# A decoder layer's attended values divided through row-step DMAs instead of PE transposes, with every engine's order rewritten

## What is computed

```python
attn = jax.nn.softmax(scores, axis=-1)                       # self: 112 keys, cross: 375 keys
out = jnp.einsum('bhqk,bkhd->bqhd', attn, V).reshape(b, s, H * hd)
x1 = _layernorm(x + out @ Wo.T + bo)                         # after the self attention
...
xq = fp4_quant_dequant(x2); wq = fp4_quant_dequant(w)        # blocks of 16, scale = max|x| / 6
```

## Time and profile before

| what | value |
|---|---|
| median of 3 runs | 660.07 us (658.95 to 660.67) |
| the profiled execution | 659.02 us |
| its span | 657.2 us |
| granted PE clock, mean | 0.97 of full speed |
| busy: PE, DVE, ACT, POOL | 583.8, 494.2, 292.3, 222.1 us |
| DMA moved | 69.61 MB, mean 106 GB/s |
| packets | 65568 |

### The profile page before, as it was taken

One profiled execution on the slowest core, in us unless ns is written; L12 is line 12 of the kernel. 1 busy time (PEld: TensorE's weight loads), 2 busy tenths in 40 slices (PEclk: granted clock), 3 DMA queues, 4 the chain that ended last, 5 costly groups with the idle time before them and its releaser, 6 DMA issues.

```text
span 657.2 us, 16127 instructions
## 1 busy us (share of the span) xinstructions
PE 583.8 (89%) x5602; PEld 372.0 (57%) x5602; DVE 494.2 (75%) x1475; ACT 292.3 (44%) x703; POOL 222.1 (34%) x280
## 2 busy tenths in 40 slices
PE   3677898898999999999999999989999999887874
PEld 3444566465566666666665656565666655554542
DVE  3598889876969687786969685668788696968662
ACT  1333365554445455445545454545545454433411
POOL 4533235242332515052524325151505252403100
PEclk9998899998999999999999999999999999996996
DMA  7554554345152435353352335362535341220000
GB/s 223 163 173 123 137 158 130 103 104 143 45 140 80 135 88 144 104 143 104 86 151 69 112 89 143 105 162 74 141 98 145 96 98 48 57 82 1 16 9 16
DMA packets 65568, 69.61 MB, mean 106 GB/s; under 512 B 11008, under 2 KB 57040, under 8 KB 65488
## 3 DMA queue, kind: packets, MB, share of 16 engines
q1 hardware_dynamic: 63248, 66.23, 37.0%
q10 hardware_dynamic: 2240, 2.35, 1.1%
HBM read 39.72 MB, written 27.00 MB: 102 GB/s over the span
## 4 chain that ended last, share of the span: by engine, by line
PE 36%; issue 26%; DVE 19%; POOL 13%; ACT 3%; DMA 2%; SPq 0%; DVEq 0%; POOLq 0%; ACTq 0%
PE misc L2230 10%; POOL move_a L702 4%; POOL move_x L702 4%; PE misc L2326 3%; PE prob L2164 3%; DVE junk L1402 3%; PE misc L2258 3%; PE score L2150 3%; PE xpv L2205 3%; PE misc L2279 2%; PE misc L2216 2%; PE prob L2159 2%; POOL rstd L707 2%; DVE amax L1394 2%; DVE qt L1316 2%
## 5 line engine op out<-in xcount | busy, mean ns | idle before, releaser
L1402 DVE CUSTOM_DVE_ANT_0 junk<-score,maskbias 112x375 bf16<-112x375 f32 x256 | 130.1, 546 | 60.5 <-PE score L2150 56.4
L887 ACT ACTIVATE xP<-prob 128x448 f32<-128x448 f32 (+1 forms) x192 | 95.3, 541 | 80.6 <-PE prob L2164 73.5
L707 POOL TENSOR_TENSOR rstd<-veps,half 128x1 f32<-128x1 f32 (+1 forms) x44 | 28.1, 638 | 277.3 <-DVE veps L1485 277.2
L702 POOL TENSOR_TENSOR move_a<-mT,negeye 16x448 bf16<-16x448 f32 x64 | 64.3, 1023 | 79.5 <-ACT mT L847 79.5
L702 POOL TENSOR_TENSOR move_x<-mT,negeye 16x448 bf16<-16x448 f32 x64 | 64.8, 1030 | 54.7 <-ACT mT L847 54.6
L2230 PE MATMUL misc<-wguT,xqT 128*128 128x352 f32 x224 | 73.5, 462 | 1.1 <-ACT xqT L847 1.1
L2164 PE MATMUL prob<-move_x,shift_x 128*128 128x448 bf16 x192 | 54.4, 362 | 1.0 <-POOL move_x L702 1.0
L2230 PE MATMUL misc<-xwvT_s,ctxT_s 128*128 128x256 f32 (+1 forms) x192 | 53.5, 402 | 1.9 <-DVE ak_parts L1421 1.7
L2230 PEld LDWEIGHTS misc<-wguT,xqT 128*128 128x128 f32 x224 | 41.9, 191 | 22.1 <-issue 1.9
L2150 PE MATMUL score<-xK,xQ 64*128 64x375 f16 x256 | 43.7, 332 | 12.1 <-DVE xmax L1402 10.9
L2258 PE MATMUL misc<-ctxT_s,xwkT_s 128*128 128x375 f32 x128 | 48.4, 501 | 1.8 <-DVE ak_parts L1421 1.4
(11 more groups left out here) (163 smaller groups left out, 1084.9 us busy)
## 6 DMA issues: line engine op xcount, KB each, us to landing
xk_dram<-xk_parts SPq DMA_DIRECT2D x64, 192.0 KB, 3.2
xK<-xk_dram SPq DMA_DIRECT2D x16, 768.0 KB, 4.5
ctxT_s<-in_ctxT SPq DMA_DIRECT2D x15, 375.0 KB, 3.4
ak_dram<-ak_parts SPq DMA_DIRECT2D x64, 64.0 KB, 2.1
aq_dram<-aq_parts SPq DMA_DIRECT2D x64, 64.0 KB, 2.1
aK<-ak_dram SPq DMA_DIRECT2D x16, 256.0 KB, 2.9
aQ<-aq_dram SPq DMA_DIRECT2D x16, 256.0 KB, 3.8
xq_dram<-xq_parts SPq DMA_DIRECT2D x64, 64.0 KB, 2.1
```

Of the source, the lines that this page charges most:

```text
L702: pool.tensor_tensor(dst[0:H, heads, :], mT[:, n].unsqueeze(1).to_broadcast([H, GH, S]), negeye[:, heads].unsqueeze(2).to_broadcast([H, GH ...
L707: pool.tensor_tensor(rstd[rows_of(n), n], veps[rows_of(n), n], half[rows_of(n)], ALU.pow).then_inc(rstd_ready[n], 1)
L887: act.activation(xP[0:KEYS[c], g % 2, c], prob[m][0:KEYS[c], 0:GH * S].rearrange("p (h q) -> p h q", h=GH), ACT.Exp).then_inc(probs.taken[ ...
L1402: dve.tensor_tensor_reduce(junk[:, m], score[m][0:S, 0:SC], maskbias[:], 1.0, -3.0e38, ALU.add, ALU.max, xmax[:, b.par, h:h + 1]).then_inc ...
```

## The change

Both attentions divide in another place. V's tiles interleave value columns and ones (`0:VW:2`), so that in `aoT` and `xoT` even rows hold values and odd rows hold sums. `aoT` and `xoT` have one buffer instead of two. A new step `spread` on SP's queue copies, with four DMAs per batch and attention, the odd rows to `den` and the even rows to `num`, 64 partitions of 896 bytes each, SBUF to SBUF. Both tiles are then in the row order in which the projection wants its input, with the output weights and the value bias reordered on the host to match. `invert` takes the reciprocal of the whole `den` tile on VectorE (128 x 224), and `attend` multiplies `num` and `den` on GpSimd into `aattT` or `xattT`. `turn_out`, `turn_att`, `normalise` and ScalarE's copies behind them are gone. `layernorm(f)` on VectorE gets a wait on the down product two tiles earlier. The lists of all engines, and the table of the `misc` ring, are written anew in ramp, slot and drain.

```diff
+            def spread(b, n):
+                src, ready = ((aoT, aoT_ready), (xoT, xoT_ready))[n]
+                sp.wait_ge(ready, b.times(1, 1))
+                wait_if(sp, att_ready[n], b.times(1, 0))
+                for odd, dst, landed in ((1, den[n], den_in[n]), (0, num[n], num_in[n])):
+                    for e in range(2):
+                        sp.dma_start(dst[HALF * e:HALF * e + HALF], src[odd:P:2, DT * e:DT * e + DT]).then_inc(landed, 16)
...
+            def attend(b, n):
...
+                pool.wait_ge(num_in[n], b.times(32, 32))
+                pool.wait_ge(inverted[n], b.times(1, 1))
+                pool.tensor_tensor(dst, num[n][:], den[n][:], ALU.mult).then_inc(att_ready[n], 1)
...
-            def normalise(i, b, n, label, part):
-                m = miscs.wait_full(dve, i, label)
-                v = misc[m][0:S].rearrange("p (h d) -> p h d", h=H)
-                if part == 0:
-                    c_norm[n].done(dve.reciprocal(rsum[:, n], v[:, :, HD]))
-                    return
-                c_norm[n].wait(dve, b)
-                dve.tensor_tensor(att[:, n], v[:, :, 0:HD], rsum[:, n].unsqueeze(2).to_broadcast([S, H, HD]),
-                                  ALU.mult).then_inc(miscs.taken[m], 1)
+            def invert(b, n):
+                dve.wait_ge(den_in[n], b.times(32, 32))
+                dve.reciprocal(den[n][:], den[n][:]).then_inc(inverted[n], 1)
...
-                copy(aV[:, b.par, :, 0:HD], misc[m][0:S, 0:D].rearrange("p (h d) -> p h d", h=H)).then_inc(miscs.taken[m], 1)
+                copy(aV[:, b.par, :, 0:VW:2], misc[m][0:S, 0:D].rearrange("p (h d) -> p h d", h=H)).then_inc(miscs.taken[m], 1)
...
             def layernorm(b):
+                if b.c > 1:
+                    miscs.wait_taken(dve, tile_slot(b.c - 2) + 1, "down")
...
-            def turn_att(i, which, n):
-                turn(i, f"{which}.att", att[:, n].rearrange("p h d -> p (h d)"), range(DT), D, after=(f"{which}.out",))
             def project_self(i, b):
-                project_rows(i, "A.o", lambda c: aattT[:, c], lambda c: woT_s[:, c], S, D, after=("A.att",))
+                pe.wait_ge(att_ready[0], b.times(1, 1))
+                project_rows(i, "A.o", lambda c: aattT[:, c], lambda c: woT_s[:, c], S, D)
...
-MISC_ORDER = ["hT1", "q", "hT0", "down", "v", "A.mT", "k", "X.xT", "gate0", "up0", "gate1", "up1", "A.out", "K0",
-              "A.att", "A.o", "V0", "X.out", "K1", "X.att", "V2", "X.o", "A.xT", "X.mT", "A.q", "V1"]
+MISC_ORDER = ["v", "k", "q", "hT1", "hT0", "A.mT", "down", "X.xT", "gate0", "up0", "gate1", "up1", "K0", "A.o",
+              "V0", "K1", "V2", "V1", "X.o", "A.xT", "X.mT", "A.q"]
```

More of the change, by code:

```diff
@@ L794, in slot @@
                 diagonal(i, a, 2, False)
+                diagonal(i, a, 3, False)
                 residual(a)
-                diagonal(i, a, 3, False)
+                attend(a, 0)
                 power(0, a)
-                keep_x1(a)
-                shifts(0, a)
                 if ft:
@@ L802, in slot @@
                     shifts(2, ft)
+                shifts(0, a)
+                attend(ct, 1)
+                keep_x1(a)
                 diagonal(i, c, 0, True)
@@ L828, in drain @@
                 diagonal(at[15], at[15], 3, True)
+                attend(at[14], 1)
+                keep_x1(at[15])
                 power(1, at[12])
@@ L831, in drain @@
                 shifts(2, at[10])
+                attend(at[15], 1)
+                power(1, at[13])
                 power(2, at[11])
                 shifts(2, at[11])
-                keep_x1(at[15])
-                power(1, at[13])
                 power(2, at[12])
@@ L956, in take @@
                 copy(dst, misc[m][:, 0:n * w].rearrange("p (t s) -> p t s", t=n)).then_inc(miscs.taken[m], 1)
-            def attended(i, b):
-                lo = b.c % (RING + 1) * S
-                take(i, "X.att", xattT[:, :, lo:lo + S])
             def tanh(i, b, u):
@@ L2524, in ramp @@
-                turn_out(at[3], at[2], "X.out", xoT, xoT_ready)
-                scores_cross(at[3], at[3], 4)
-                turn_att(at[3], "A", 0)
-                turn_att(at[3], "X", 1)
-                project_self(at[3], at[4])
+                ctx_v(at[3], at[4], 2)
+                project_self(at[3], at[4])
+                front(at[3], at[5], "q")
+                scores_cross(at[3], at[3], 3)
+                project_cross(at[3], at[1])
+                ctx_v(at[2], at[3], 2)
+                scores_cross(at[3], at[3], 4)
@@ L2599, in slot @@
                 scores_cross(i, c, 6)
+                ctx_k(i, kv, 0)
+                project_self(i, a)
                 ctx_v(i, kv, 0)
-                turn_out(i, ct, "X.out", xoT, xoT_ready)
                 ctx_k(i, kv, 1)
                 scores_cross(i, c, 7)
-                turn_att(i, "X", 1)
                 ctx_v(i, kv, 2)
+                ctx_v(i, kv, 1)
                 if xo:
@@ L2636, in drain @@
                 scores_cross(at[14], at[14], 1)
+                pv_self(at[14], at[15], 1)
                 turned_cross(at[14], at[13], 1, 1)
-                down(at[14], at[9])
-                pv_self(at[14], at[15], 1)
                 scores_cross(at[14], at[14], 2)
+                ctx_v(at[14], at[15], 0)
                 turned_cross(at[14], at[13], 1, 2)
-                turn_out(at[14], at[15], "A.out", aoT, aoT_ready)
                 scores_cross(at[14], at[14], 3)
-                gate_up(at[14], at[10], "gate", 1)
@@ L2656, in drain @@
-                scores_cross(at[14], at[14], 7)
-                ctx_k(at[14], at[15], 1)
-                turn_att(at[14], "X", 1)
-                turn_max(at[14], at[14], "X.mT", xmax)
-                project_cross(at[14], at[11])
+                ctx_k(at[14], at[15], 1)
+                turn_xq(at[14], at[10])
+                scores_cross(at[14], at[14], 4)
+                project_self(at[14], at[15])
+                gate_up(at[14], at[10], "gate", 0)
+                scores_cross(at[14], at[14], 5)
```

1376 lines of the change are left out of this document (678 added, 698 removed), and 14 rows, old and new, of tables (MISC_IN, MISC_OUT).

## The result

The changed kernel took 673.99 us (median of 4 runs, 671.72 to 676.34), the kernel before 660.37 beside it. The ratio is 1.02, with a 95% interval of 1.0139 to 1.026: slower by about 2%, where 652.5 was forecast. It lies outside the range of 637 to 671.

A forecast was written before the change was run, and what follows sets the result against it. It took PE to bound the slots, with chains in the drain. From a span of 657.2 us it took 3 for slots, 3 for ramp, 1.5 for drain: 649.7, forecast as a 652.5 median, range 637 to 671.

The forecast's parts named there:

- What leaves PE: Slots: PE loses its transposes, 1.79 us a slot, leaving 33.8 us of PE work without any new hole.
- The reciprocal: VectorE: each new reciprocal of 224 columns takes 1.54 us, two a slot.
- GpSimd's product: GpSimd: each of two new 128 x 224 products a slot takes 0.8 us.
- The DMAs: SP's queue: eight more DMAs a slot; sums are there 3.2 us after ScalarE's copy, landing 2.6 after issue.
- The self chain: Slot, pv_self 1 to project_self: product done at 7.7 us, PE there at 7.4, so PE waits 0.3.
- The cross chain: Slot, project_self to project_cross: xattT takes 6.2 us against PE's 5.6, so PE waits 0.6 to 0.7.
- The quantizing run: Slot, VectorE's nine quant_x steps beside GpSimd's diagonals: tile at 12.1 us, PE at turn_xq at 11.5, wait 0.65.
- rival 2: Port shared by GpSimd and VectorE: products take 1.46 us instead of 0.8, slot 37.4, kernel about 674; chance 0.27.
- Ramp and drain: Before and after the slots: ramp -3 us, between -8 and +7; drain -1.5, between -7 and +9.
- Rival 3: SP's queue: row-step DMAs land 1.5 us late behind the gets, slot 36.9, kernel about 661; chance 0.08.
- Rival 1: Slots: the holes close because VectorE is ahead, slot 34.6, kernel about 638; chance 0.25.
- Edits with one answer: Single buffers, layernorm's earlier wait, V copies with a step of two, GpSimd's later diagonals: all cost nothing.

The follow-up runs named there:

- v2: Changed kernel, slots only: turn_xq behind second cross score pair, first cross maxima between quantizing steps 6 and 7, GpSimd's cross product before self LayerNorm's shifts; 654.74 us.
- mid0: v2 without its GpSimd edit, so the cross product stands behind the self LayerNorm's shifts as in the changed kernel; 655.25 us.
- actdiag: Changed kernel with each slot's four self diagonals moved from GpSimd to ScalarE, as 16 products of one head each; 668.44 us.
- the short reciprocals: Two measuring kernels, the changed kernel and v2, each with reciprocals of 16 columns instead of 224, most sums not inverted; 666.49 and 644.21 us.
- attend_dve: Changed kernel with the product of values and inverted sums on VectorE directly behind each reciprocal, none on GpSimd; 682.37 us.
- recip16: Changed kernel with reciprocals of 16 columns instead of 224, leaving most sums not inverted, a measuring kernel only; 666.49 us.

## Why the prediction was wrong, point by point

**What leaves PE: right.** 33.67 us busy in a slot at full clock, 33.8 forecast. Over the kernel PE's busy time fell only 11.6 us, not 29: the sum also counts the matmuls that ran at the lower clock (35.1 to 35.2 us in slots 5, 6 and 8, at 0.96).

**The reciprocal: right.** 1.547 us against 1.54. The Trainium skill's page "VectorE: DVE Perf Modes", section "First, the fixed hardware budget", led to 1.98; the trace does not agree, and the line through the two shorter rows was the better guide.

**GpSimd's product: right.** 0.67 and 0.69 us against 0.8.

**The DMAs: right, a little early.** Landing 1.9 to 2.2 us after issue (2.6 forecast from a larger copy). ScalarE's copy ends at 359.69; the second transfer of sums, issued at 360.4, is there 2.7 us after it, against 3.2. VectorE takes them only at 363.91. SP's row and the page's median:

```profile
359.83 1.15 SPq L531 DMA_DIRECT2D aden<-aoT  x2
```

```profile
aden<-aoT SPq DMA_DIRECT2D x32, 56.0 KB, 1.9
```

**The self chain: right.** Inversion 5.0 us after pv_self 1's end at 358.9 (5.2 forecast), product done at 7.3 (7.7), PE there at 7.4 (7.4). No wait, against 0.3.

**The cross chain: right.** A wait of 0.71 against 0.6 to 0.7. v2 against mid0 shows the named cause: with the product ahead of the shifts it is 0.2.

**The quantizing run: the step that failed.** It forecast the tile at 12.1 us after the slot's start, PE at 11.5, a wait of 0.65. Measured: tile at 14.2, PE at 12.3, wait 2.0. Two parts were mis-sized, both by the same thing. Three steps were counted as stretched by GpSimd where five were (four beside the diagonals, one beside the residual's sum): 2.9 us more instead of 2.0 (4.7 against actdiag's 1.8). And VectorE came to the run 0.9 late, at 7.6 instead of 6.65. The trace shows a likely reason, which no run tests by itself: the last quantizing steps of the feed-forward's hidden tile (`quant_h`) run beside the cross diagonals (0.98 and 1.14 us, where the same forms took 0.22 and 0.51 elsewhere in that slot). The remaining 0.3 of the 2.1 us is the LayerNorm and the nine steps without any stretch, 3.8 instead of 3.45. PE was 0.8 late itself, by the next hole, which is why its wait grew by 1.35 and not by 2.1. The mechanism had its rows, and rival 2 even named it; but I used it for the products that the change adds and not, at full size, for the steps that it moves.

**A hole without a term.** The k product of the next batch waited 0.86 us for a bank that xq_lo_ frees, behind those same stretched steps, and turn_max 0.42. The forecast had 0.7 for all small waits; they were 1.3. With turn_xq's 1.35 more and 0.3 less at project_self this makes 37.7 out of 36.1.

**The clock: missing.** The forecast had no term for it, though PE's granted clock in the drain of before is below 1.00 in the same rows where PE has holes. A hole of 2 us costs its own 2, and in some slots 1.5 more (slot 8 against slot 7).

**Ramp and drain.** +5.4 (+6.8 by the slot's first instruction) against -3, and -7.4 against -1.5; the first is inside its bounds of -8 to +7, the second just past its lower one of -7. The ramp's term missed two things. 7.0 us of VectorE's work were set off against 6.9 of PE's, and the short reciprocals show a part of VectorE's share on the path, 2.75 to 6.3 us for some 9.5. And PE's share did not come back: its busy time in the ramp is 144.8 us for 142.5, at a granted clock of 0.90 for 0.96. How the 5.4 divides between the two stays open. In the drain the wait of 7.2 us in three places that PE had for hq before is 1.3 now, in one place.

**Rivals.** Rival 2 gave 674 and 37.4 a slot, and 674.0 and 37.7 came. That the totals agree is luck: it had +10 for the ten slots and nothing for the drain, where 18 to 19 and -7.4 came. Its place was wrong too: the products took 0.67, not 1.46, and attend_dve, which takes them off GpSimd, is no faster in the slots. It was right that VectorE is slowed beside GpSimd, and wrong on which instructions matter. The range was too narrow by the prediction's own chances: rival 2 had 0.27, and its 674 lay outside the 637 to 671 that were to hold 8 in 10. Rival 3 (late DMAs) did not happen. Rival 1 did not come either; mid0 and v2 show how far it was: with turn_xq later and one pair of maxima earlier the slot is 36.3, with GpSimd's product earlier too 35.7, where the rival had 34.6.

**Edits with one answer.** V's copies with a step of two are not quite the same: 402 ns for 368 (aV), 396 for 384 (xV). ScalarE is busy 17.8 of 37.7 us in a slot, and no run shows that these few nanoseconds matter.

What stays open: why nearly equal holes at turn_xq (1.9 to 2.0 us) are followed by a fall of the clock in some slots and not in others of one and the same run. In the changed kernel's profile the clock fell in slots 5, 6, 8 and 9 and not in 7, 12 and 13 (39.1 and 37.7 above); recip16's slot 8 has the same hole at 1.00.

## What to carry to other kernels

When a change puts steps in a new order, price every step by who runs beside it in the new order, not by its old mean; here five unchanged instructions took 2.9 us more in a slot, while 3.1 us of new ones were nearly hidden. Where there is a choice, put work that reads PSUM, which kept its time here, beside GpSimd's, and steps from SBUF to SBUF elsewhere. And if moving a late wait on the waiting engine only moves the wait, go to the list of the engine that is late.

## What the runs showed of the hardware

- VectorE's steps of 128x256 in SBUF take 0.29, 0.23, 0.43, 0.42, 0.42 us alone (actdiag). Beside GpSimd's diagonals of only 16 partitions the first four take 0.94, 0.84, 1.06, 1.04, even those with one tensor input and 16-bit data; beside its sum of 112x256 the fifth takes 0.83. The self maxima, which read PSUM and of which one pair in slot 8 stands beside two cross diagonals, keep their time (ns min/median/max over the ten slots of the changed kernel):

```profile
L1439 DVE TENSOR_REDUCE amax<-score x40: 607/614/625, 187.2 to 529.7; 112x4 f32<-112x448 f32 x40
```

- A reciprocal in float32 takes 252 ns for 16 columns, 426 for 44, 1547 for 224: 6.2 ns a column on a fixed 150 ns, the same slope over the whole range.
- A power of GpSimd takes 36.06 us for 128x224, 161 ns a column, where one column takes 0.56.
- ScalarE takes 0.29 us from one product of 16x112 to the next (0.37 for one by itself), so that 16 of them (4.66 us) cost it more than the four of GpSimd (3.83) that they replace.
- DMAs of 56 KB from SBUF to SBUF with a partition step of two land in 1.9 to 2.2 us.
